# Experts' rows gathered into two buffers, edges counted in pairs, and the first expert's weights split a stage earlier

## What is computed

```python
h = gat_layer(x, W1, a_src1, a_dst1, b1, src, dst, heads=8, out_c=96, concat=True)
h = jax.nn.elu(h)
out = gat_layer(h, W2, a_src2, a_dst2, b2, src, dst, heads=1, out_c=768, concat=False)
...
glog = xf @ Wg + bg                      # 4 groups, the best 2
elog = jnp.einsum('nd,gde->nge', xf, We) + be   # 8 experts in each, the best 4
combine = gw[:, :, None] * ew
for g in range(G):
    h = jax.nn.gelu(jnp.einsum('nd,edm->enm', xf, W1[g]) + b1[g][:, None, :], approximate=False)
    o = jnp.einsum('enm,emd->end', h, W2[g]) + b2[g][:, None, :]
    y = y + jnp.einsum('end,ne->nd', o, combine[:, g, :])
```

## Time and profile before

| | us |
|---|---|
| median of 3 runs (1604.42 to 1613.96) | 1612.75 |
| the profiled execution | 1607.04 |
| its span, first to last instruction | 1604.9 |
| TensorE busy | 1379.4 (86%) |
| VectorE busy | 1114.2 (69%) |
| ScalarE busy | 744.7 (46%) |
| GpSimd busy | 503.4 (31%) |

### The profile page before, as it was taken

The page is one execution under the profiler, slowest core; times in us unless marked ns, Lnnn a source line. Parts: engine busy times, 40 slices in busy tenths (PEclk is TensorE's granted clock), DMA queues, the critical chain, the costliest instruction groups (busy, mean ns, idle before and its releaser), DMA issues. The chain is left out here.

```text
span 1604.9 us, 29908 instructions
## 1 busy us (share of the span) xinstructions
PE 1379.4 (86%) x7608; PEld 1131.7 (71%) x7609; DVE 1114.2 (69%) x1707; ACT 744.7 (46%) x1136; POOL 503.4 (31%) x551
## 2 busy tenths in 40 slices
PE   6878878787777759799946999999999999889996
PEld 4645545633322229799935998999998999888886
DVE  5479989899999968758866455444464645676772
ACT  3465565344444433412215454444454535555662
POOL 1000000003334400032323445454554545454453
PEclk9999999799999979999967999999999999999998
DMA  4300001142221224244468788777787877899864
GB/s 162 130 17 9 17 23 62 35 152 71 89 68 60 64 57 131 60 119 112 127 147 294 210 208 216 181 167 166 174 206 193 214 179 181 235 250 276 234 158 84
DMA packets 100290, 222.11 MB, mean 138 GB/s; under 512 B 15052, under 2 KB 54220, under 8 KB 100120
## 3 DMA queue, kind: packets, MB, share of 16 engines
q1 hardware_dynamic: 77304, 140.99, 27.1%
q0 software_dynamic: 22160, 78.22, 23.9%
q10 hardware_dynamic: 784, 2.36, 0.4%
HBM read 161.86 MB, written 55.75 MB: 136 GB/s over the span
## 5 line engine op out<-in xcount | busy, mean ns | idle before, releaser
L913 PE MATMUL ps_o<-prob,h_head 128*97 128x512 f32 (+1 forms) x480 | 190.5, 536 | 56.0 <-DVE prob L856 56.0
L1928 POOL DMA_INDIRECT out_nodes<-y,to_index x92 | 165.7, 1802 | 220.8 <-DMA out_nodes<-y,to_index 177.2
L2068 DVE TENSOR_TENSOR e_xt_lo<-ps_xt,e_xt_hi 128x768 fp32r<-128x768 f32 x92 | 88.1, 958 | 165.6 <-ACT e_xt_hi L2016 165.2
L2190 PE MATMUL ps_h<-e_hi,e_xt_hi 128*128 (+1 forms) x546 | 195.0, 357 | 2.3 <-DVE e_xt_lo L2068 1.6
L913 PEld LDWEIGHTS ps_o<-prob,h_head 128*97 128x97 f32 x480 | 74.4, 167 | 172.5 <-issue 92.3
L2169 PE MATMUL ps_y<-e_hi,e_ht_hi 128*128 (+1 forms) x546 | 191.9, 352 | 2.0 <-DVE e_ht_lo L2108 2.0
L2190 PE MATMUL ps_h<-e_lo,e_xt_hi 128*128 (+1 forms) x546 | 185.3, 339 | 0.0
L2190 PE MATMUL ps_h<-e_hi,e_xt_lo 128*128 (+1 forms) x546 | 184.9, 339 | 0.0
L2169 PE MATMUL ps_y<-e_hi,e_ht_lo 128*128 (+1 forms) x546 | 184.4, 338 | 0.0
L2169 PE MATMUL ps_y<-e_lo,e_ht_hi 128*128 (+1 forms) x546 | 184.2, 337 | 0.0
L2080 DVE TENSOR_TENSOR e_lo<-raw,e_hi (+1 forms) x192 | 178.0, 952 | 8.5 <-ACT e_hi L2024 8.5
(11 more groups left out here) (317 smaller groups left out, 3065.2 us busy)
## 6 DMA issues: line engine op xcount, KB each, us to landing
raw<-in_ew SPq DMA_DIRECT2D x192, 384.0 KB
w_room<-rel_dram SPq DMA_DIRECT2D x14, 640.0 KB, 4.4
b_all<-in_eb SPq DMA_DIRECT2D x32, 192.0 KB
al_src<-al_dram SPq DMA_DIRECT2D x1, 5000.0 KB, 14.7
xs<-in_x SPq DMA_DIRECT2D x5, 768.0 KB, 12.9
x_in_t<-in_x SPq DMA_DIRECT2D x10, 384.0 KB, 3.6
out_nodes<-x SPq DMA_DIRECT2D x10, 384.0 KB, 4.1
table<-xf SPq DMA_DIRECT2D x10, 384.0 KB, 2.7
```

Of the source, the lines that this page charges most:

```text
L913: turn = nc.tensor.matmul(ps_o[u][0:C1 + 1, c, 0:WID[c]], h_head[:, u, t, :], prob[:, t % 2, 512 * c:512 * c + WID[c]], start=(t == 0), st ...
L1928: nc.gpsimd.indirect_dma_start(out, bass.IndirectOffsetOnAxis(to_index[:, w:w + 1], 0), y[:, w, :], None, bounds_check=ROWS - 1, compute_o ...
L2068: nc.vector.tensor_tensor(xt_lo[:, :, :].rearrange("p (b k) n -> p b (k n)", b=2), ps_x[:, :, 0:HALF], xt_hi[:, :, :].bitcast(F32).rearran ...
L2190: summed = nc.tensor.matmul(ps_h[:, 0:HID], a, b[:, bass.ds(e % 2, 1), c * HID:(c + 1) * HID] .rearrange("p o m -> p (o m)"), start=(c == ...
```

## The change

Four parts. In **features** the `span_col` transpose moves ahead of the twelve matmuls. In **counting** a loop body now handles two pairs of edge tiles, so the number of pairs per node tile is rounded up to an even one; 1252 columns are counted in place of 1280, the narrow piece first, and the sums are closed with one column each. ScalarE makes both pairs' `away` before the first `one_dst`. In **routing** the first expert's W1 is split, the third expert's list is made, and expert 1's weights are loaded; the last two `add_bias` move to the experts' block. In **experts** rows land in `landing` (two buffers), VectorE copies them to `in_rows` (`keep_rows`), GpSimd gathers the rows of tile k+3 in its round k and not those of k+2, `turn_x` and the head's list stand behind the first product, which uses the high parts first, and the second product is no longer cut in two.

```diff
@@ EP, AHEAD @@
-EP = -(-EDGES // (2 * P))
+EP = -(-EDGES // (2 * P)) + 1
-AHEAD = 4
+AHEAD = 5
@@ node_features, tensor: the transpose that ends the edge ranges @@
                 last.then_inc(pe_edges, 1)
+                pe.wait_ge(edge_step, 3)
+                nc.tensor.transpose(ps_m[0:1, 0:2 * NT], span_col[:, :],
+                                    s.ident[0:2 * NT, 0:2 * NT]).then_inc(pe_edges, 1)
                 pe.wait_ge(w1t_kept, KD)
...
                 last.then_inc(pe_wa, 1)
-                pe.wait_ge(edge_step, 3)
-                nc.tensor.transpose(ps_m[0:1, 0:2 * NT], span_col[:, :],
-                                    s.ident[0:2 * NT, 0:2 * NT]).then_inc(pe_edges, 1)
@@ transform_and_count @@
+        USED = -(-N // 4) * 4
+        SHARES = ((1024, USED - 1024), (0, 512), (512, 512))
-            return eng.Fori(first, end)
+            return eng.Fori(first, end, 2)
@@ scalar @@
+                        for pair in range(2):
+                            act.wait_ge(dst_made, m + (pair + 1))
+                            for q in range(2):
+                                last = nc.scalar.activation(away[:, pair, q, :], s.column[:, t * P:(t + 1) * P],
+                                                            ACT.Abs, bias=s.dst_neg[:, bass.ds(2 * e + 2 * pair + q, 1)])
+                            last.then_inc(away_made, 1)
+                        for pair in range(2):
+                            act.wait_ge(away_made, m + (pair + 1))
+                            if pair:
+                                act.wait_ge(onehot_used, m + 2)
+                            nc.scalar.activation(one_dst[:, slot, pair].rearrange("p o q n -> p (o q n)"),
...
@@ tensor @@
-                    for c, (at, width) in enumerate(PARTS):
-                        last = nc.tensor.matmul(ps_c[:, c, 0:width], zeros[:, :], zeros[:, 0:1].broadcast_to([P, width]),
-                                                start=False, stop=True)
...
+                    for c in range(3):
+                        last = nc.tensor.matmul(ps_c[:, c, 0:1], zeros[:, :], zeros[:, 0:1], start=False, stop=True)
@@ mix_and_route, sync: after the last store_gates @@
+                for piece in range(3):
+                    sp.wait_ge(s.w1_in[piece], 16)
+                    load_first(sp, s, w1, 1, piece)
...
@@ mix_and_route, gpsimd: after the first gather @@
-                add_bias(NT - 2, bias_added[0])
-                add_bias(NT - 1, s.scattered)
-                pool.wait_ge(bias_added[0], 16 * (NT // 2))
-                pool.wait_ge(bias_added[1], 16 * (NT // 2 - 1))
-                pool.wait_ge(s.scattered, 16)
@@ mix_and_route, scalar @@
+                act.wait_ge(mixed, NT)
+                for piece in range(3):
+                    act.wait_ge(s.w1_in[piece], 16)
+                    at = piece * PIECE
+                    nc.scalar.activation(s.e1_hi[:, 0, at:at + PIECE], s.raw1[:, 0, at:at + PIECE],
+                                         ACT.Copy).then_inc(w1_hi_made, 1)
@@ mix_and_route, vector @@
                 rest_of_gates(NT - 2)
+                rest_of_weights(0)
                 start = dve.value_load(s.starts[0:1, 1:2], min_val=LEAD, max_val=LIST - NT)
                 keep(1, start)
+                match(2)
                 rest_of_gates(NT - 1)
+                rest_of_weights(1)
...
+                keep(2, start)
+                rest_of_weights(2)
@@ run_experts, gpsimd, one tile @@
-                    pool.wait_ge(x_lo_made, next_x)
-                    pool.wait_ge(gathered, 16 * k + 32)
-                    keep_gates(k + 1).then_inc(gate_kept, 1)
-                    next_index(k + (LEAD + 2)).then_inc(index_set, 1)
+                    pool.wait_ge(gathered, pool.snap(arrived))
+                    keep_gates(k + 2, u).then_inc(gate_kept, 1)
+                    pool.wait_ge(ready, 1)
+                    pool.wait_ge(x_lo_made, next_x)
+                    next_index(k + (LEAD + 3)).then_inc(index_set, 1)
                     pool.wait_ge(ready, 1)
-                    pool.wait_ge(turned, after_x)
-                    pool.wait_ge(index_set, after_x)
-                    pool.wait_ge(gate_kept, after_x)
-                    gather()
+                    pool.wait_ge(rows_kept, after_x)
+                    pool.wait_ge(index_set, far_x)
+                    gather(1 - u)
@@ run_experts, vector @@
                     split_x(k + 1)
+                    keep_rows(k + 2)
...
+                def keep_rows(k):
+                    dve.wait_ge(gate_kept, k + 1)
+                    nc.vector.tensor_copy(rows[:, :], landing[:, bass.ds(k % 2, 1), 0:D]
+                                          .rearrange("p o d -> p (o d)")).then_inc(rows_kept, 1)
@@ run_experts, tensor, turn_x and one tile @@
-                    pe.wait_ge(gathered, 16 * k + 16)
+                    pe.wait_ge(rows_kept, k + 1)
...
                     if head:
-                        if not last:
-                            pe.wait_ge(rows_made, e + 1)
-                            list_tokens(nc, s, ps_l).then_inc(listed, 1)
...
+                    turn_x(k + 1)
+                    if head and not last:
+                        pe.wait_ge(rows_made, e + 1)
...
+                        list_tokens(nc, s, ps_l).then_inc(listed, 1)
...
                     if not start:
                         pe.wait_ge(w2_lo_made, 3 * e if head else 3 * e + 3)
-                        down(k, u, (0,))
-                    turn_x(k + 1)
-                    if not start:
-                        down(k, u, (1,))
+                        down(k, u, 0)
+                        down(k, u, 1)
```

More of the change, by code:

```diff
@@ L1377, in _ @@
                 sp.wait_ge(pad_out, 32)
-                for piece in range(3):
-                    sp.wait_ge(s.w1_in[piece], 16)
-                    sp.wait_ge(s.w2_in[piece], 16)
             @block.gpsimd
@@ L1899, in _ @@
                 load_bias(sp, s, b1, 0)
-                for e in range(1, WRING):
+                sp.wait_ge(b1_in, 16)
+                load_bias(sp, s, b1, 1)
+                for e in range(2, WRING):
                     load(e)
@@ L2007, in _ @@
                 pool.reg_mov(free, 16 * n + 32)
-                last = pool.snap(free)
-                pool.wait_ge(gathered, last)
-                pool.wait_ge(scattered, last)
+                pool.wait_ge(scattered, pool.snap(free))
+                pool.reg_mov(arrived, 16 * n + 48)
+                pool.wait_ge(gathered, pool.snap(arrived))
             @block.scalar
@@ L2088, in tile @@
                         weights(e + 1, 0, (0, 1))
+                    if start:
+                        keep_rows(k + 1)
                     dve.wait_ge(h_summed, k + 1)
@@ L2208, in tile @@
                     last_t.then_inc(h_turned, 1)
-                pe.wait_ge(third_made, 1)
-                list_tokens(nc, s, ps_l).then_inc(third_listed, 1)
                 turn_x(0)
                 n = over_tiles(pe, "pe_tiles", tile)
-                down(n, (E - 1) % 2, (0, 1))
+                for half in range(2):
+                    down(n, (E - 1) % 2, half)
 def program(nc, x, edge_src, edge_dst, w1, att1, bias1, w2, w2_t, att2, bias2, wg, we, bg, be, ew1, eb1, ew2, eb2, out):
@@ L2294, in program @@
             s.raw_room = sb("raw_room", [P, 2 * WRING * ROW], where=routing)
+            s.e1_room = sb("e1_room", [P, 2 * 2 * ROW + 2 * TW], where=routing, side="right")
             s.b1_all = sb("b1_all", [P, BRING, HID], where=routing)
```

220 lines of the change are left out of this document (136 added, 84 removed).

## The result

| | before | changed |
|---|---|---|
| median | 1610.83 us (4 runs, 1604.42 to 1613.96) | 1564.43 us (4 runs, 1562.03 to 1567.72) |
| ratio | | 0.9718, 95% interval 0.9682 to 0.9755 |
| span of the profiled execution | 1604.9 | 1563.1 |

The forecast was 1585 with a range from 1566 to 1604: the direction was right, and the time fell by 46 us where 28 were expected.

What follows compares the result with a forecast made beforehand. In the experts, TensorE's waits for gathered rows and list one-hots, and the chain of scatters, were taken as the bounds. 2 + 6 + 7 + 13 = 28 us off 1607.0 gave 1579, as a median 1585; range 1566 to 1604.

Steps and rivals of the forecast that it cites:

- What bounds the kernel: Opening step, on the experts: a tile waiting for nothing takes 7.52 us; scatter steps of 7.99 and 8.56 us are longer.
- Costed at nothing: Experts and start: the row copy, the second product in one piece, high parts first and the W1 split cost 0 us.
- Rows ahead: Experts: gathering rows ahead lets TensorE run further ahead of the scatters and saves 13 us, bounds 4 and 31.5.
- A and C: Experts' stretches near start (923.9 to 1043.7 us) and end (1368.5 to 1548.3), where scatters set the step; 8.8 us gain together.
- The step of the scatters in C: Sign to look for in the experts' late stretch: time between successive scatters stays near 8.5 us.
- Features: Features stage: moving the transpose ahead of twelve matmuls removes TensorE's 1.89 us idle; -2 us, bounds 1.5 and 2.
- Counting: Counting stage: 96 pairs at 1.30 us against 88 bodies at 1.54, with closing, ScalarE and VectorE terms; -6 us in sum.
- The start of the experts: Experts' start: first product near 846, first scatter at 865, eighth scatter 6 to 7 us sooner; 6.6 us, bounds 1 and 11.
- All waits go: Rival, chance 0.08: scatters land sooner too and all the experts' waits go; 50 us off, 1562.
- The scatters set everything: Rival, chance 0.18: the experts' scatter chain starts no earlier and the lead doesn't grow; 12 us off in all, 1601.
- pairs cost: Rival, chance 0.11: in counting, rounding up to even pairs wins, +9 us for -6; 1600.
- The copy against GpSimd: Rival, chance 0.07: in 43 chained experts' steps the copy collides with gather and scatter issues, 1.4 us each; +60, 1645.

Runs made afterwards that it cites:

- e2: Changed kernel with TensorE's old order in all tiles but the first (list ahead of first product, turn between halves of second product): 1582.74 us, ratio 0.9818.
- e7: Changed kernel, but the first product waits for the low part at its start and takes the parts in turn as before: 1566.06 us, ratio 0.9729.
- e8: Changed kernel with high parts still first, but list and turn back in their old places: 1571.25 us, ratio 0.9760.
- e13: Changed kernel with in effect one landing buffer, the gather waiting for one more copy of rows: 1570.44 us, ratio 0.9762.
- e5: Changed kernel loading only an eighth of the weights' bytes from the fourth expert on: 1545.91 us, ratio 0.9592.
- e6: Kernel before the change, loading only an eighth of the weights' bytes from the fourth expert on: 1580.56 us, ratio 0.9814.
- e15: The changed kernel itself, measured and profiled once more: 1565.68 us, ratio 0.9726.
- e3: Changed kernel with the whole counting stage of before: 1571.32 us, ratio 0.9751.
- e10: Changed kernel with counting's x_lo made by GpSimd and not VectorE: 1565.86 us, ratio 0.9726.
- e12: Changed kernel with VectorE copying the landed rows twice each time, first into an unread buffer: 1568.29 us, ratio 0.9733.

## Why the prediction was too small, step by step

**What bounds the kernel: one sentence failed.** "A tile that waits for nothing takes 7.52 us" was read from PE's row, where the modelled end of the transposes covers a wait of 0.24 to 0.27 us for `e_xt_lo`. The chain of the earlier trace rows went from product to product and didn't show it either; the wait is in the list of PEld. The unhindered tile is 7.25 us.

**"Costed at nothing": the order of the products.** This is the failed step. The second product in one piece and the high parts first are indeed the same 36 matmuls, but the turn's place decides when the low part is there, and the list's place whether TensorE waits for VectorE's one-hots at a head. With landing buffers the order is worth 18 us (e2), as much as the forecast fell short between medians; half of it alone is enough for the 0.27 us (e7, e8). The prediction also put the waits for lists into the share of the rows gathered ahead. e2 has the rows ahead and still waits 13.1 us for lists: it is the list's place that removes them.

**Rows ahead: right in size, in part by luck.** 13 forecast, 13.7 by e2's trace, which is one execution against another, with some 6 us of play. The working behind it is only partly borne out: it rested on how far a lead can grow, 4.4 us at A and C each; e2 shows 6.4 and 3.3. And e13 shows that the second landing buffer adds 5 us at most.

**The step of the scatters in C "still near 8.5": wrong.** It is 7.98 us, and 7.95 to 8.23 in the other kernels with the whole of the new order. Scatters do follow one another there without a pause, so it is the landings that got shorter: 7.50 us in the mean before, 6.98 in the changed kernel, 6.98 to 7.21 in those variants. Of this, 0.2 us lie in the issue, with which a landing is counted: 1.89 us in the mean in C before, 1.69 in the changed kernel. With the old order (e2) the landing is still 7.43 and the step 8.41, near the forecast, so most of the drop came with the new order. The prediction took the landing for given. e5 and e6 show that weights in flight lengthen it; in C 14 of 21 scatters took over 7 us before, 10 of 21 in the changed kernel. Why a quicker TensorE makes the same loads meet fewer scatters was not settled: the bytes are the same.

**Features: 1.5 to 2 us forecast, about 2 shown.** TensorE's 1.89 us went, as expected: the first `ps_x<-ident,xn` follows L335 at once. In the profiled execution of the changed kernel the block of L335 took longer, at a granted clock of 0.74 from 24.0 to 27.4 us, where it was 1.00 before. The whole block in the kernel before (the product behind it is in the earlier trace rows, at 32.42), then block and product in the changed kernel, and in the changed kernel once more (e15):

```profile
22.51 7.91 PE L332 MATMUL ps_al<-w_t,att_diag 128*16 128x384 f32 x24 [0.66 <-ACT w_t L273]
...
22.04 9.61 PE L335 MATMUL ps_al<-w_t,att_diag 128*16 128x384 f32 x24
31.58 1.53 PE L299 MATMUL ps_x<-ident,xn 128*128 128x128 f32 x12
...
21.90 7.92 PE L335 MATMUL ps_al<-w_t,att_diag 128*16 128x384 f32 x24
29.74 1.53 PE L299 MATMUL ps_x<-ident,xn 128*128 128x128 f32 x12
```

From the block's start to that product it is 9.9 us before, 9.5 in the ledger's execution and 7.8 in e15. The block took 7.9 us in ten of the fourteen profiled executions that have this part of the change and 9.6 in four, the ledger's among them. That is why the ledger shows only 0.5 us ahead of counting.

**Counting: 6 forecast, 4.7 in the trace, 4 to 7 between medians and ratios (e3).** The sign and the pair were right (1.26 us for 1.30). The prediction gave VectorE +4 for being close to TensorE's pace. What the traces show in its place are four node tiles of 23.5 us for 22.8, about 3 us in all, each with a stretch at a granted clock of 0.50, of which the kernel before has none from 70 to 275 us. The mean granted clock in this stage is 0.92, and 0.97 before.

**The start of the experts: 6.6 forecast, 4.1 seen.** The first product came at 840.2, 16.5 us earlier and earlier than the 846 forecast, and the first scatter at 862.2 (865 forecast). The next rows held it back: the second gather's gates stand behind the two bias adds (846.39), and the third gather (848.19) took 9.2 us.

```profile
846.39 0.77 POOL L1965 COPY gate<-landing 128x32 f32<-128x32 f32 x1
...
848.19 1.11 POOL L1958 DMA_INDIRECT landing<-table,index  x1 [0.90 <-DMA out_nodes<-bias_rows,node_i]
857.60 0.21 POOL L1965 COPY gate<-landing 128x32 f32 x1 [8.30 <-DMA landing<-table,index]
...
858.02 0.56 DVE L2189 COPY in_rows<-landing 128x768 f32 x1 [5.00 <-POOL gate L1965]
```

**The rivals.** "All waits go" (1562, at 0.08) is the nearest in time. The waits of the earlier trace rows did go and landings did get shorter, as it said, but its 11 us for the start came to 4.1, and what removed the waits for lists and part of the landings was the order, which it didn't name. "The scatters set everything" and "pairs cost" didn't happen. The copy against GpSimd: see below; at 1.4 us a step it was far off, since GpSimd's gather waits for this very copy and its scatter waits for a landing. One sign that the prediction named did appear: the issues of gathers are visibly longer, 1.35 us in the mean for 1.09. It was not the copy that lengthened them but the instructions with two inputs that VectorE does right behind it.

## What to carry to other kernels

Before a tile is called free of waits, the weight loads' row is to be read beside TensorE's: a wait that ends under the modelled tail of the matmuls before shows only there. Moving a step earlier on one engine pays only where the engine that must answer is free to: on a queue with a fixed order (here scatter before gather) the same move cost 33 us, and a copy of 0.56 us that takes the buffer out of the ring turned it into 18 us of gain. Before an engine is named as what sets a repeated step, the repeats are to be compared with one another and with the granted clock in each: here the ones with a stretch at the lower clock were the long ones, and a run that took work from VectorE took these stretches away too. The cheaper parts of a change (fewer columns, a short close) should be tried alone. And two profiled executions of one kernel should be laid side by side before a ledger is read to the microsecond.

## What the runs showed of the hardware

A VectorE copy with one input in SBUF and a GpSimd copy do get into each other's way. In the changed kernel an index copy of one element, 0.2 us elsewhere, ran beside the copy of the rows:

```profile
1201.44 0.56 DVE L2189 COPY in_rows<-landing 128x768 f32 x1 [1.42 <-POOL gate L1965]
...
1201.52 0.53 POOL L1954 COPY index<-list_i 128x1 int32 x1 [0.28 <-issue]
```

The page's groups show the issues of the changed kernel, scatter and gather; 1802 and 1090 ns were their means before. An issue of a gather takes 1.07 us by itself and up to 2.36 beside VectorE's instructions with two inputs in SBUF (`e_lo`, the one-hots of a list). What counts is which began first: 41 gathers of the changed kernel began while one of these was running and took 1.68 us in the mean (2 before the change), and 25 during whose issue one began took 1.09. Of the scatters, 27 began so and took 1.88 (before, 41 and 2.06), the others 1.60. Beside `e_xt_lo`, which has one of its inputs in PSUM, they stayed at 1.60.

```profile
L1969 POOL DMA_INDIRECT out_nodes<-y,to_index x92 | 154.5, 1679 | 217.9 <-DMA out_nodes<-y,to_index 184.1
L1958 POOL DMA_INDIRECT landing<-table,index x93 | 125.3, 1347 | 82.7 <-DVE in_rows L2189 40.1
```

```profile
1435.08 1.49 DVE L1231 TENSOR_TENSOR one_row<-lanes,row_in_tile 128x1280 f16<-128x1280 bf16 x1
...
1435.15 2.36 POOL L1958 DMA_INDIRECT landing<-table,index  x1 [0.90 <-DVE in_rows L2189]
```

e10 shows the other direction, VectorE's one-input instructions held by one of GpSimd's. The Trainium skill (SBUF — State Buffer, section "Who interferes with whom") says this of one pair of ports that either engine holds for a whole instruction, and the rows agree for copies and one-input instructions in both directions. They don't show that it matters here: a second copy in every tile (e12) costs 1 to 4 us.
